# A recurrence kernel's first pass: one unit less between a pair's transposes and its steps, with the prologue's small work moved

## The chip, the cores and the metric

The kernel runs on one core of a Trainium2 chip. The metric is the time of one execution on the device in microseconds (us), the median of repeated runs.

## The reference

The input x is 8 sequences of 1024 tokens with 256 features. Six modulation rows per sequence come from `silu(c) @ wmod` (`sa, ca, ga, sb, cb, gb`). The kernel must compute:

```python
h = layernorm(x) * (1 + ca) + sa
xb = einsum('bsd,ed->sbe', h, B)
# step, over 1024 tokens:
h_t = tanh(h_{t-1} @ A.T + xb_t);  y_t = h_t @ C.T
x = x + ga * layernorm_affine(y + h)
h = layernorm(x) * (1 + cb) + sb
# gated recurrence over 64 groups: f, i = sigmoid(...), g = tanh(...), c = f * c + i * g
x = x + gb * tanh(h @ wo.T + c_final @ uo.T + bo)
```

## The kernel before

Each sequence is cut into 16 chunks of 64 tokens, which gives 128 rows (8 sequences by 16 chunks). One step of the recurrence advances all 128 rows by one token. Tokens go in pairs (`PAIRS` = 32). The first pass handles them in numbered units, and each unit works on several pairs at once, as a pipeline written out by hand in `unit1` of every engine. Engines run their queues in order, and semaphores with counts join them.

For unit number `ref` in the kernel before:

- DVE (VectorE) takes the mean and variance of pair `ref`, and subtracts and scales pair `ref-1` (`hin<-xin,mvA,uvec`, L1071). POOL (GpSimd) works out the reciprocal deviation (L637, L639). ACT (ScalarE) multiplies by it (L808). POOL adds `sa` (L646).
- PE (TensorE) transposes pair `ref-2` into a bank (`psT` or `psC`, L1452), ACT copies pair `ref-3` from its bank, rounded, into `hi` (L784), DVE puts the rest into `lo` (L1083).
- PE multiplies pair `ref-4` by B in twelve matmuls (`times_b`, L1435), in two halves of the accumulators `psWR` or `psOF`. ACT copies the sums to `state` (`xb`, L795).
- PE adds the two steps of pair `ref-R1LAG` (`recur1`, L1400) to the sums, four matmuls a step, and ACT takes the tanh (L763). `R1LAG` is 5, so pair 0 has its first step in unit 5.

A unit on PE is: first step, `times_b`, second step, transposes. Pairs 23 to 31 and the first chunks run in a different order: from unit 28 on (`ahead`), steps are done by `summed` (L1475 on PE, L825 on ACT). ACT then also rounds both steps' results with `high` (`hsh<-hs`, L842), and DVE takes the remainder (`low`, `hsl<-hs,hsh`, L1101). In units 28 and 32 to 35 the eight later weights are transposed as well (`LATE1`, `late`): four transposes on PE (L1361), a copy on ACT (L754), a remainder on DVE (L1029). The second pass follows (`unit2`, `step` at L1489, `project` at L1516), on the same PE queue.

The prologue makes the tables: `ca` and `sa` in two matmuls each (L1335), the weights `B`, `A` and `C` (L1361, L749, `weight_low` at L989), and the other two thirds of the modulation in `batch_rows(1)` and `batch_rows(2)` (L1344, 8 rows by 512 columns, copied by ACT at L811 and L787). SP's queue starts all loads in the order of `FIRST`.

Of the kernel before, what the change touches and what calls it, by code (L numbers as in the profile page):

```python
# [20 lines left out]
def adaln_kernel(nc, x, A, B, C, gamma, beta, wf, uf, bf, wi, ui, bi, wc, uc, bc, wo, uo, bo, in_c, cond, wmod, out):  # L21
# [7 lines left out]
    P = 128  # L29
# [20 lines left out]
    PEELED = 18  # L50
    RAW = 12
    THREE = 8
# [16 lines left out]
    LATE1 = {28: (0,), 32: (1,), 33: (2, 3), 34: (4, 5), 35: (6, 7)}  # L69
# [23 lines left out]
    with ctx:  # L93
# [69 lines left out]
        def htok(p):  # L163

            return hin[:, p % 3 if p < THREE else p % 2, :]

# [27 lines left out]
        def bank(name):  # L194
# [7 lines left out]
        BANK = {"B": psI, "A": psG, "C": psI}  # L202
# [3 lines left out]
        q_table = sem("q_table")  # L206
        q_w = {n: sem("q_w_" + n) for n in EARLY + LATE}
# [37 lines left out]
        a_park = [sem(f"a_park{i}") for i in range(2)]  # L245
        a_park3 = [sem(f"a_park3_{i}") for i in range(3)]
# [77 lines left out]
                    *a_x, *a_xp, a_stats, a_mv, a_ve, a_rstd, a_tmp, a_h, *a_park, *a_park3, a_T, a_hT,  # L324
# [9 lines left out]
        def ranges(cuts, end):  # L334
            return list(zip(cuts, cuts[1:] + [end]))

        RUNS1 = ranges([*range(PEELED), *range(RP1, UNITS1)], UNITS1)

# [114 lines left out]
        def _(sp):  # L453
# [31 lines left out]
            def unit1(v, ref):  # L485
# [4 lines left out]
                if has(ref, 2, PAIRS):  # L490
                    sp.wait_ge(a_h, v.lin(2, -2))
                    p = pair1(v, ref, 2)
                    sp.dma_start(h_park[bass.ds(p * 2, 2), :, :].rearrange("t p d -> p t d"),
                                 two(htok(ref - 2))).then_inc(a_park3[(ref - 2) % 3] if ref - 2 < THREE else a_park[ref % 2], 16)
# [92 lines left out]
            with sp.Fori(0, left) as r:  # L587
# [4 lines left out]
                for i in range(3):  # L592
                    sp.wait_ge(a_park3[i], 16 * len(range(i, THREE, 3)))
                for i in range(2):
                    sp.wait_ge(a_park[i], 16 * ((PAIRS - THREE) // 2))
# [144 lines left out]
        def _(act):  # L740
# [29 lines left out]
            def unit1(v, ref):  # L770
                rec, ahead = has(ref, R1LAG, RP1), ref >= RP1 + R1LAG
                p = ref - RP1 - R1LAG
                if rec:
                    tanhs(v, 0)
                if ref in LATE1:
                    late(LATE1[ref][0])
                if ahead:
                    summed(2 * p)
# [6 lines left out]
                if ref == 4:  # L785
                    act.wait_ge(q_mod, 4)
                    act.activation(mods[:, 2:4, :], psO[0:NB, :].rearrange("b (i d) -> b i d", i=2), ACT.Copy).then_inc(q_col, 1)  # L787
                if has(ref, 4, RP1) or has(ref, 4 + RP1 + AP, PAIRS - RP1 - AP):
                    act.wait_ge(a_B, v.lin(1, -3))
                    if ref - 4 < RP1:  # L790
                        sums = (psWR, psOF)[ref % 2][:, :].rearrange("p (m n) -> p m n", m=H)[:, :, 0:D]
                        xb = row(pair1(v, ref, 4)).rearrange("p (m n) -> p m n", m=H)
                    else:
                        sums, xb = (psW, psO)[ref % 2][:, :], row(pair1(v, ref, 4))
                    act.activation(xb, sums, ACT.Copy).then_inc(a_xb, 1)  # L795
# [13 lines left out]
                if ref == 3:  # L809
                    act.wait_ge(q_mod, 3)  # L810
                    act.activation(mods[:, 0:2, :], psF[0:NB, :].rearrange("b (i d) -> b i d", i=2), ACT.Copy).then_inc(q_col, 1)  # L811
                if ref in (1, 3, 4):
                    weight({1: "B", 3: "A", 4: "C"}[ref])
# [152 lines left out]
        def _(dve):  # L966
            dve.wait_ge(q_ident, 7)
# [3 lines left out]
            def prepare():  # L971
# [60 lines left out]
            def unit1(v, ref):  # L1032
# [19 lines left out]
                if norm:  # L1052
                    dve.wait_ge(a_stats, v.lin(2))
                    if ref >= 2:
                        dve.wait_ge(a_ve, v.lin(1, -1))
                    apart(dve)
                    for tt in range(2):
                        dve.bn_aggr(mv[:, tt, :], st[:, tt, :]).then_inc(a_mv, 1)
                    pair = ref - 1
                    if 3 <= pair < THREE:  # L1060
                        dve.wait_ge(a_T, pair - 2)
                    if pair >= THREE:
                        dve.wait_ge(a_T, v.lin(1, -2))
                    if 3 <= pair < THREE + 2:
                        last = max(p for p in range(min(pair, THREE)) if p % 3 == (pair % 3 if pair < THREE else pair % 2))
                        dve.wait_ge(a_park3[last % 3], 16 * (last // 3 + 1))
                    elif pair >= THREE:
                        dve.wait_ge(a_park[(ref - 1) % 2], v.half(16, 1, -8 * THREE))
# [22 lines left out]
                if ref == 5:  # L1091
                    weight_low(1, "C")
                if ref == 9:
# [234 lines left out]
        def _(pe):  # L1328
            pe.wait_ge(q_ident, 7)
# [9 lines left out]
            def batch_rows(j):  # L1339

                pe.wait_ge(q_wm[f"wm{j}"], 16)
                pe.wait_ge(q_scT, 2)
                for k in range(H):
                    last = pe.matmul((psF, psO)[j - 1][0:NB, :], scT[:, k, :], wm[j][:, k, :], start=(k == 0), stop=(k == H - 1))  # L1344
                last.then_inc(q_mod, 1)

            def batch_columns():

                pe.wait_ge(q_col, 2)
                pe.wait_ge(q_whi, 2)  # L1350
# [14 lines left out]
            def weight(name):  # L1365
                if name == "C":
                    pe.wait_ge(q_whi, 1)
                    pe.wait_ge(q_wlo, 1)
# [13 lines left out]
            def prepare():  # L1382
# [21 lines left out]
            def unit1(v, ref):  # L1404
# [6 lines left out]
                if rec:  # L1411
                    if ref == R1LAG:
                        pe.wait_ge(q_col, 2)
# [4 lines left out]
                def times_b():  # L1418
                    back = 4
                    if not has(ref, back, PAIRS):  # L1420
                        return
                    if ref == back:
                        pe.wait_ge(q_whi, 1)
                        pe.wait_ge(q_wlo, 1)
                    pe.wait_ge(a_hT, v.lin(1, 1 - back))
                    for n in range(3 * H * H):
                        if n == 1:
                            pe.wait_ge(a_hl, v.lin(1, 1 - back))
                        m, k = n // (3 * H), n // 3 % H
                        w, h = ((whi, hmT_hi), (whi, hmT_lo), (wlo, hmT_hi))[n % 3]  # L1430
                        if ref - back < RP1 + AP:
                            ps = sums1(ref - back)[m][:, 0:2 * P]
                        else:
                            ps = (psW, psO)[(ref - back) % 2][:, m * 2 * P:(m + 1) * 2 * P]
                        last = pe.matmul(ps, w["B"][:, k, m * P:(m + 1) * P],  # L1435
                                         h[:, (ref - back) % 2, k * 2 * P:(k + 1) * 2 * P],
# [300 lines left out]
```

## Time and profile before

| what | value |
|---|---|
| median of 3 runs | 567.37 us (567.2 to 567.86) |
| profiled execution, own time | 567.14 us |
| its span in the trace | 565.3 us |
| PE busy | 545.3 us, 96% |
| DVE busy | 382.4 us, 68% |
| ACT busy | 341.2 us, 60% |
| POOL busy | 341.6 us, 60% |

The profiled execution takes 1.84 us more than its span, and the median is 0.23 us above it. "Busy" is the share of the span in which an engine has an instruction in work. A PE that is always busy has no gap between matmuls, and then time can only come from work that is removed or run at a higher clock. PEld is the loading of weights into the array, which runs beside the matmuls. In names, `out<-in` gives the tiles written and read, and L with a number is a line of the kernel.

### The profile page before, as it was taken

The numbers are of one execution on the slowest core, as the hardware profiler recorded it, in microseconds if no ns is written. First come the engines' busy times: TensorE is split into PE (matmuls) and PEld (weight loads), VectorE is DVE, ScalarE is ACT, GpSimd is POOL, SyncE is SP. The second block draws the span as 40 slices with busy tenths as digits, with TensorE's granted clock in tenths as the row PEclk, the third lists the DMA queues.
The fourth block names the chain that finished last, engine by engine and source line by source line (L and its number), as shares of the span: only waits on it lengthen the run. The fifth ranks groups of instructions, "written<-read, shape, count | busy, mean of one in ns | idle before, by whom it ended". The sixth has DMA issues, their size and how long they took to land.

```text
span 565.3 us, 13418 instructions
## 1 busy us (share of the span) xinstructions
PE 545.3 (96%) x4616; PEld 533.8 (94%) x4616; DVE 382.4 (68%) x908; ACT 341.2 (60%) x862; POOL 341.6 (60%) x475
## 2 busy tenths in 40 slices
PE   5999999999989999999999999999999999999992
PEld 2899999999989999999999999999999999999992
DVE  6889888886757655555766666666666677666762
ACT  3777777775456555564665556666655557567550
POOL 4667777660466444354766666677666667677353
PEclk9999999999999999999999999999999999999997
DMA  8566445434243222212233333433333343232334
GB/s 277 157 194 195 150 149 150 134 93 157 89 131 112 67 71 76 70 66 76 66 103 100 106 101 92 123 111 102 95 94 95 94 134 110 76 121 68 86 94 148
DMA packets 58513, 64.09 MB, mean 113 GB/s; under 512 B 5408, under 2 KB 49736, under 8 KB 58448
## 3 DMA queue, kind: packets, MB, share of 16 engines
q1 hardware_dynamic: 58448, 63.26, 36.8%
q8 instruction: 36, 0.59, 0.4%
q14 instruction: 29, 0.24, 0.1%
HBM read 46.44 MB, written 16.81 MB: 112 GB/s over the span
## 4 chain that ended last, share of the span: by engine, by line
PE 86%; POOL 3%; issue 3%; ACT 2%; DVE 2%; DMA 1%; SPq 1%; POOLq 0%; DVEq 0%; ACTq 0%
PE psI L1530 14%; PE psOF L1530 14%; PE psG L1530 13%; PE psWR L1584 7%; PE psWR L1489 7%; PE psWR L1400 4%; PE psWR L1435 4%; PE psOF L1435 4%; PE psOF L1400 3%; PE psOF L1516 3%; PE psC L1516 3%; PE psT L1563 2%; PE psT L1452 1%; PE psC L1452 1%; DMA tA<-rows_d 1%
## 5 line engine op out<-in xcount | busy, mean ns | idle before, releaser
L646 POOL TENSOR_TENSOR hin<-hin,uvec 128x256 f32<-128x256 f32 x64 | 50.7, 813 | 32.5 <-ACT hin L808 32.5
L653 POOL TENSOR_TENSOR hsl<-hs,hsh 128x512 fp32r<-128x512 f32 x24 | 30.9, 1287 | 52.2 <-DVE state L1245 31.6
L881 ACT ACTIVATE psOF<-psOF,biasT 128x256 f32<-128x256 f32 x64 | 25.9, 444 | 56.4 <-PE psOF L1530 56.4
L1229 DVE SCALAR_TENSOR_TENSOR lo<-psT,cb1T,hi 128x256 fp32r<-128x256 f32 x60 | 26.3, 479 | 46.4 <-ACT hi L873 46.4
L1117 DVE TENSOR_TENSOR pre<-psWR,state 128x256 f32<-128x256 f32 x44 | 18.6, 424 | 47.7 <-PE psWR L1489 47.7
L1489 PE MATMUL psWR<-hs,AT 128*128 128x128 f32 x368 | 49.7, 275 | 1.0 <-ACT hs L835 1.0
L660 POOL TENSOR_TENSOR xin<-xin,tA 128x512 f32<-128x512 f32 x32 | 41.5, 1298 | 13.5 <-DMA tA<-rows_d 13.5
L687 POOL TENSOR_TENSOR zn<-zn,tA 128x512 f32<-128x512 f32 x32 | 41.3, 1289 | 12.1 <-ACT zn L846 12.1
L1071 DVE SCALAR_TENSOR_TENSOR hin<-xin,mvA,uvec 128x256 f32<-128x256 f32 x56 | 41.1, 772 | 9.6 <-DMA h_park<-hin 9.2
L846 ACT ACTIVATE zn<-state,nmA,rstdA 128x256 f32<-128x256 f32 x64 | 35.0, 595 | 20.5 <-POOL nmA L677 20.5
L1489 PEld LDWEIGHTS psWR<-hs,AT 128*128 128x128 f32 x368 | 45.3, 191 | 1.4 <-ACT hs L835 1.2
L682 POOL TENSOR_TENSOR wx<-wx,tG 128x512 f32<-128x512 f32 x24 | 36.4, 1518 | 11.0 <-ACT wx L905 10.8
L700 POOL TENSOR_TENSOR wx<-wx,uvec 128x512 f32<-128x512 f32 x24 | 31.0, 1293 | 14.7 <-DVE state L1245 12.6
L846 ACT ACTIVATE xn<-state,nmB,rstdB 128x256 f32<-128x256 f32 x64 | 34.8, 590 | 5.2 <-POOL nmB L709 5.0
L881 ACT ACTIVATE gg<-psG,biasT 128x256 f32<-128x256 f32 x64 | 27.0, 474 | 16.6 <-PE psG L1530 16.6
L835 ACT ACTIVATE hs<-pre 128x256 f32<-128x256 f32 x44 | 18.3, 417 | 29.7 <-DVE pre L1117 29.5
L1530 PE MATMUL psI<-hi,wiT_hi 128*128 128x256 f32 x120 | 35.9, 299 | 0.0
L881 ACT ACTIVATE psI<-psI,biasT 128x256 f32<-128x256 f32 x64 | 26.0, 445 | 14.9 <-PE psI L1530 14.9
L808 ACT ACTIVATE hin<-hin,rstdA 128x256 f32<-128x256 f32 x64 | 28.7, 498 | 9.8 <-POOL rstdA L639 9.8
L1530 PE MATMUL psOF<-hi,wfT_hi 128*128 128x256 f32 x120 | 33.5, 279 | 1.1 <-DVE gf L1165 1.1
L1530 PE MATMUL psI<-lo,wiT_hi 128*128 128x256 f32 x120 | 33.3, 278 | 0.0
L1530 PE MATMUL psOF<-lo,wfT_hi 128*128 128x256 f32 x120 | 33.3, 278 | 0.0
(351 smaller groups left out, 2303.8 us busy)
## 6 DMA issues: line engine op xcount, KB each, us to landing
h_park<-hin SPq DMA_DIRECT2D x32, 256.0 KB, 2.2
hin<-h_park SPq DMA_DIRECT2D x64, 128.0 KB
xin<-in_L_attn_x_dram SPq DMA_DIRECT2D x64, 128.0 KB
tA<-rows_d SPq DMA_DIRECT2D x32, 256.0 KB, 4.5
out_dram<-state SPq DMA_DIRECT2D x64, 128.0 KB
xin<-in_L_attn_x_dram SPq DMA_DIRECT2D x28, 256.0 KB, 2.9
tW<-rows_d SPq DMA_DIRECT2D x32, 128.0 KB, 4.0
tG<-rows_d SPq DMA_DIRECT2D x24, 128.0 KB, 4.0
```

Source lines behind the costliest of these rows:

```text
L646: pool.tensor_tensor(h, h, sa, ALU.add).then_inc(a_h, 1)
L660: pool.tensor_tensor(xg, xg, both(tA[:, m % 2, D:W]), ALU.add).then_inc(s_xg, 1)
L682: pool.tensor_tensor(t, t, both(gb_of(o)), ALU.mult).then_inc(s_ob, 1)
L687: pool.tensor_tensor(two(zn[:, :]), two(zn[:, :]), both(tA[:, m % 2, 0:D]), ALU.mult).then_inc(s_zg, 1)
L846: act.activation(dst[:, j * D:(j + 1) * D], tiles_of(m)[:, j, :], ACT.Identity, bias=nm[:, j:j + 1], scale=rstd[:, j:j + 1]).then_inc(done, 1)
L881: act.activation(dst[:, m * POS:(m + 1) * POS], src[:, m * POS:(m + 1) * POS], fn, bias=biasT[:, i, m, n % NB:n % NB + 1]).then_inc(done, 1)
L1071: dve.scalar_tensor_tensor(halfw(dst, tt), halfw(src, tt), mv[:, tt, 0:1], ca1, ALU.subtract, ALU.mult).then_inc(a_tmp, 1)
L1400: ins = pe.matmul(sums1(v.c - R1LAG)[m][:, tt * P:(tt + 1) * P], AT[:, k, m * P:(m + 1) * P], hs[:, k, :, 1 - tt, :], start=False, stop=(k ...
L1435: last = pe.matmul(ps, w["B"][:, k, m * P:(m + 1) * P], h[:, (ref - back) % 2, k * 2 * P:(k + 1) * 2 * P], start=(n % (3 * H) == 0), stop= ...
L1489: ins = pe.matmul(ps, AT[:, k, m * P:(m + 1) * P], hs[:, k, :, (t - 1) % 4, :], start=(k == 0 and (separate or m == 0)), stop=(k == H - 1 ...
L1530: last = pe.matmul(ps[:, at + m * columns:at + (m + 1) * columns], w[name][:, k, m * P:(m + 1) * P], xx[:, k, :], start=(start and n == 1) ...
L1584: last = pe.matmul(ps[:, j * D:(j + 1) * D], h[:, k, j * P:(j + 1) * P], w["wo"][:, k, :], start=(n < HELD and c == 1 and j == 0), stop=(c ...
```

## The change

`R1LAG` becomes 4: `times_b` and the first step move one unit towards the transposes. Pair `ref-3` is now copied by ACT, completed by DVE and multiplied by PE in the same unit, and the first pass has 35 units in place of 36. `times_b` does the eight matmuls that read `hi` first and the four that read `lo` last. ACT's order in a unit changes. The first pair's means are taken ahead of the wait for `ca`. All pairs use three `hin` buffers, so the loop that covered units 17 to 22 is written out. `batch_rows(1)` moves from unit 2 to 3, `batch_rows(2)` from 3 to 7, the weight C from unit 4 to 6, `batch_columns` from 8 to 9, and the small tables on DVE from units 6 to 15 to units 9 to 18. Seven matmuls without a use (`busy`) are added in the prologue. The weight A is loaded ahead of the two thirds.

```diff
-    R1LAG = 5
-    UNITS1 = PAIRS + 4
+    R1LAG = 4
+    UNITS1 = PAIRS + 3
...
-    FIRST = ["cond", "ca", "x0", "sa", "B", "x1", "x2", "wm1", "A", "x3", "wm2", "x4", "C", "x5"]
+    FIRST = ["cond", "ca", "x0", "sa", "B", "x1", "x2", "A", "wm1", "x3", "x4", "C", "x5", "wm2"]
...
-    LATE1 = {28: (0,), 32: (1,), 33: (2, 3), 34: (4, 5), 35: (6, 7)}
+    LATE1 = {27: (0,), 31: (1,), 32: (2, 3), 33: (4, 5), 34: (6, 7)}
...
-            return hin[:, p % 3 if p < THREE else p % 2, :]
+            return hin[:, p % 3, :]
...
# ACT, unit1
-                if rec:
-                    tanhs(v, 0)
                 if ref in LATE1:
                     late(LATE1[ref][0])
-                if ahead:
-                    summed(2 * p)
                 if has(ref, 3, PAIRS):
...
                     act.activation(hmT_hi[:, b, :], (psT, psC)[b][:, :], ACT.Copy).then_inc(a_hT, 1)
...
+                if ref == 3:
+                    weight("A")
+                if rec:
+                    tanhs(v, 0)
                 if ahead:
-                    summed(2 * p + 1)
-                    high(p)
-                if rec:
-                    tanhs(v, 1)
-                if ref == RP1 + R1LAG - 1:
-                    starts()
+                    summed(2 * p)
                 if has(ref, 1, PAIRS):
...
+                if has(ref, 3, RP1) or has(ref, 3 + RP1 + AP, PAIRS - RP1 - AP):
...
+                    act.activation(xb, sums, ACT.Copy).then_inc(a_xb, 1)
+                if rec:
+                    tanhs(v, 1)
+                if ahead:
+                    summed(2 * p + 1)
+                    high(p)
+                if ref == RP1 + R1LAG - 1:
+                    starts()
...
+                if ref in (4, 8):
+                    i = (4, 8).index(ref)
+                    act.wait_ge(q_mod, 3 + i)
+                    act.activation(mods[:, 2 * i:2 * i + 2, :], psI[0:NB, :].rearrange("b (i d) -> b i d", i=2), ACT.Copy).then_inc(q_col, 1)
...
# DVE
+            dve.memset(pre[:, :], 1.0).then_inc(q_pre, 1)
...
+                dve.wait_ge(a_stats, 2)
+                apart(dve)
+                for tt in range(2):
+                    dve.bn_aggr(mv[:, tt, :], st[:, tt, :]).then_inc(a_mv, 1)
...
-                if 6 <= ref < 16:
-                    tables(ref - 6)
+                if 9 <= ref < 19:
+                    tables(ref - 9)
...
# PE
+            def busy(n):
+
+                for _ in range(n):
+                    pe.matmul(psT[:, 0:P], pre[:, 0:P], pre[:, 0:P], start=True, stop=True)
+
+            pe.wait_ge(q_pre, 1)
+            busy(4)
...
+                busy(1)
                 pe.wait_ge(q_scT, 1)
                 table("ca", psC[:, D:W], D)
+                busy(2)
                 table("sa", psO[:, 0:D], 0)
...
+                    pe.wait_ge(a_hT, v.lin(1, -2))
+                    for n, (m, w, h, k) in enumerate([(m, w, hmT_hi, k) for m in range(H) for w in (whi, wlo) for k in range(H)] +
+                                                     [(m, whi, hmT_lo, k) for m in range(H) for k in range(H)]):
+                        if n == 2 * H * H:
+                            pe.wait_ge(a_hl, v.lin(1, -2))
...
                 times_b()
+                if ref == 3:
+                    batch_rows(1)
...
                 if ref == 2:
-                    batch_rows(1)
                     weight("A")
-                if ref == 3:
+                if ref == 6:
+                    weight("C")
+                if ref == 7:
                     batch_rows(2)
-                if ref == 4:
-                    weight("C")
-                if ref == 8:
+                if ref == 9:
                     batch_columns()
```

PE's queue in the prologue, from the first pair's transposes to the first step (`psG<-ident,state` is the weight A, `psI<-ident,state` the weight C, `psOF<-state` and `psI<-state` the two thirds, `psWR<-hs,AT` the first step). Before:

```order
L1452 MATMUL psT<-ident,hin 128x128 [waits a_h]
L1452 MATMUL psT<-ident,hin 128x128
L1344 MATMUL psOF<-state 8x512 [waits q_scT,q_wm_wm1]
L1361 MATMUL psG<-ident,state 128x128 [waits q_w_A]
L1452 MATMUL psC<-ident,hin 128x128 [waits a_h]
L1344 MATMUL psOF<-state 8x512 [waits q_scT,q_wm_wm2]
L1435 MATMUL psWR<-hi,chi 128x256 [waits a_hT,q_wlo,q_whi]
L1435 MATMUL psWR<-lo,chi 128x256 [waits a_hl]
L1452 MATMUL psT<-ident,hin 128x128 [waits a_h,a_hl,a_hT]
L1361 MATMUL psI<-ident,state 128x128 [waits q_w_C,q_wlo,q_whi]
L1400 MATMUL psWR<-hs,AT 128x128 [waits q_whi,a_xb,a_end,q_col]
```

These are the rows at which a wait stands or a new group starts. After:

```order
L1453 MATMUL psT<-ident,hin 128x128 [waits a_h]
L1453 MATMUL psT<-ident,hin 128x128
L1366 MATMUL psG<-ident,state 128x128 [waits q_w_A]
L1435 MATMUL psWR<-hi,chi 128x256 [waits a_hT,q_wlo]
L1435 MATMUL psWR<-lo,chi 128x256 [waits a_hl]
L1349 MATMUL psI<-state 8x512 [waits q_scT,q_wlo,q_wm_wm1]
L1453 MATMUL psC<-ident,hin 128x128 [waits a_h]
L1406 MATMUL psWR<-hs,AT 128x128 [waits a_xb,q_whi,a_end]
```

The third pair's transposes, the weight C and the second third have left the stretch ahead of the first step, and `times_b` of the first pair now stands ahead of the first third.

ACT's queue where one unit of the `ahead` part meets the next, at the second later weight (`wiT_hi`). `hsh<-hs` is `high`, `hs<-psWR` and `hs<-psOF` are tanhs, `hi<-psT` and `hi<-psC` the copy for `times_b`. Before:

```order
L825 ACTIVATE hs<-psWR 128x8x16 [waits s_r,s_hsl]
L825 ACTIVATE hs<-psWR 128x8x16 [waits s_r]
L842 ACTIVATE hsh<-hs 128x16x32 [waits s_tanh]
L808 ACTIVATE hin<-hin,rstdA 128x256 [waits a_tmp,a_rstd]
L808 ACTIVATE hin<-hin,rstdA 128x256 [waits a_tmp]
L754 ACTIVATE wiT_hi<-psI 128x512 [waits q_lT]
L825 ACTIVATE hs<-psOF 128x8x16 [waits s_r,s_hsl]
L825 ACTIVATE hs<-psOF 128x8x16 [waits s_r]
L784 ACTIVATE hi<-psC 128x512 [waits a_B,a_T]
```

After:

```order
L820 ACTIVATE hs<-psWR 128x8x16 [waits s_r,s_hsl]
L820 ACTIVATE hs<-psWR 128x8x16 [waits s_r]
L837 ACTIVATE hsh<-hs 128x16x32 [waits s_tanh]
L750 ACTIVATE wiT_hi<-psI 128x512 [waits q_lT]
L776 ACTIVATE hi<-psT 128x512 [waits a_B,a_T]
L820 ACTIVATE hs<-psOF 128x8x16 [waits s_r,s_hsl]
L820 ACTIVATE hs<-psOF 128x8x16 [waits s_r]
L788 ACTIVATE hin<-hin,rstdA 128x256 [waits a_tmp,a_rstd]
L788 ACTIVATE hin<-hin,rstdA 128x256 [waits a_tmp]
```

The copy now stands right behind `high` and the weight's copy, ahead of the next tanh and of the scaling. It serves the `times_b` of its own unit, where it served the next unit's before.

## Rows read from the trace of the kernel before

**Rows 1.** Busy time of each engine in three stretches, PE's granted clock.
```profile
10.00:20.00 10.00, 9.53 (x40) 4.23 (x40) 9.49 (x24) 5.08 (x12) 7.27 (x12) 0.83 0.79 249
60.00:70.00 10.00, 10.00 (x90) 10.00 (x89) 8.26 (x22) 7.97 (x24) 7.06 (x11) 1.00 0.50 160
110.00:120.00 10.00, 10.00 (x90) 10.00 (x89) 8.90 (x20) 7.44 (x23) 7.59 (x12) 1.00 0.52 149
```
**Rows 2.** Chain that ended last, prologue, in order of time: start, us, what.
```profile
4.34 2.06 PE psC L1335 x4
...
7.93 0.84 POOL rstdA L639
...
10.91 0.44 PE psT L1452 x2
11.35 3.46 PE psOF L1344 x4
...
15.83 1.81 PE psOF L1344 x4
17.65 1.62 PE psWR L1435 x12
19.27 0.44 PE psT L1452 x4
19.71 0.44 PE psI L1361 x4
```
**Rows 3.** PE in short stretches of the prologue: busy, granted clock.
```profile
5.00:5.70 0.70, 0.70 (x3) 1.00 0.93 262
11.40:12.00 0.60, 0.60 (x1) 0.50 1.07 416
14.50:15.00 0.50, 0.50 (x3) 0.72 0.68 242
```
**Rows 4.** Timeline of the prologue: start, us, engine, instruction, idle before and releaser.
```profile
3.30 0.47 SPq L472 DMA_DIRECT2D xin<-in_L_attn_x_dram  x1
4.88 0.75 DVE L981 BATCH_NORM_STATS2 stA<-xin 128x6 f32<-128x256 f32 x2 [0.61 <-DMA xin<-in_L_attn_x_dram]
9.05 0.75 DVE L1046 BATCH_NORM_STATS2 stA<-xin 128x6 f32<-128x256 f32 x2
12.12 0.67 DVE L989 TENSOR_TENSOR clo<-psI,chi 128x512 fp32r<-128x512 f32 x1
14.51 0.68 DVE L1083 TENSOR_TENSOR lo<-psT,hi 128x512 fp32r<-128x512 f32 x1
```
**Rows 5.** Loads of the first 18 us: count, size, median us to landing.
```profile
xin<-in_L_attn_x_dram SPq DMA_DIRECT2D x2, 256.0 KB, 4.3
```
**Rows 6.** Timeline of a unit that starts at 64.43.
```profile
63.99 0.60 PE L1452 MATMUL psT<-ident,hin 128*128 128x128 f32 x4
64.43 1.06 PE L1400 MATMUL psWR<-hs,AT 128*128 128x128 f32 x8
65.22 0.19 PEld L1435 LDWEIGHTS psOF<-hi,chi 128*128 128x128 f32 x1
```
**Rows 7.** Timeline of an `ahead` unit that starts at 112.27.
```profile
111.83 0.60 PE L1452 MATMUL psC<-ident,hin 128*128 128x128 f32 x4
112.03 0.28 ACT L825 ACTIVATE hs<-psWR 128x128 f32<-128x128 f32 x1 [0.17 <-PE psWR L1475]
112.34 0.63 ACT L842 ACTIVATE hsh<-hs 128x512 fp32r<-128x512 f32 x1
112.88 0.89 ACT L808 ACTIVATE hin<-hin,rstdA 128x256 f32<-128x256 f32 x2
113.99 0.59 ACT L784 ACTIVATE hi<-psC 128x512 fp32r<-128x512 f32 x1
114.59 1.05 PE L1475 MATMUL psOF<-hs,AT 128*128 128x128 f32 x8
```
**Rows 8.** Timeline at two `late` weights.
```profile
122.78 0.68 DVE L1029 TENSOR_TENSOR wiT_lo<-psI,wiT_hi 128x512 fp32r<-128x512 f32 x1
123.38 0.68 DVE L1101 TENSOR_TENSOR hsl<-hs,hsh 128x512 fp32r<-128x512 f32 x1
128.38 0.60 ACT L754 ACTIVATE ufT_hi<-psI 128x512 fp32r<-128x512 f32 x1
128.87 0.59 ACT L754 ACTIVATE uiT_hi<-psG 128x512 fp32r<-128x512 f32 x1
```

More of the change, by code:

```diff
@@ L244, in adaln_kernel @@
         a_h = sem("a_h")
-        a_park = [sem(f"a_park{i}") for i in range(2)]
-        a_park3 = [sem(f"a_park3_{i}") for i in range(3)]
+        a_park = [sem(f"a_park{i}") for i in range(3)]
         a_T = sem("a_T")
@@ L334, in ranges @@
         def ranges(cuts, end):
-            return list(zip(cuts, cuts[1:] + [end]))
-        RUNS1 = ranges([*range(PEELED), *range(RP1, UNITS1)], UNITS1)
+            return list(zip(cuts, [*cuts[1:], end]))
+        RUNS1 = ranges(range(UNITS1), UNITS1)
         def walk(eng, runs, unit):
@@ L493, in unit1 @@
                     sp.dma_start(h_park[bass.ds(p * 2, 2), :, :].rearrange("t p d -> p t d"),
[L494 removed]
+                                 two(htok(ref - 2))).then_inc(a_park[(ref - 2) % 3], 16)
                 for what in LOADS.get(ref, []):
@@ L592, in _ @@
                 for i in range(3):
-                    sp.wait_ge(a_park3[i], 16 * len(range(i, THREE, 3)))
-                for i in range(2):
-                    sp.wait_ge(a_park[i], 16 * ((PAIRS - THREE) // 2))
+                    sp.wait_ge(a_park[i], 16 * len(range(i, PAIRS, 3)))
                 sp.wait_ge(a_T, PAIRS)
@@ L1051, in unit1 @@
                     late(i)
-                if norm:
+                if norm and ref >= 2:
                     dve.wait_ge(a_stats, v.lin(2))
-                    if ref >= 2:
-                        dve.wait_ge(a_ve, v.lin(1, -1))
+                    dve.wait_ge(a_ve, v.lin(1, -1))
                     apart(dve)
@@ L1058, in unit1 @@
                         dve.bn_aggr(mv[:, tt, :], st[:, tt, :]).then_inc(a_mv, 1)
+                if norm:
                     pair = ref - 1
-                    if 3 <= pair < THREE:
+                    if pair >= 3:
                         dve.wait_ge(a_T, pair - 2)
[L1062 to L1068, printed above, removed]
+                        dve.wait_ge(a_park[pair % 3], 16 * (pair // 3))
                     for tt in range(2):
@@ L1341, in batch_rows @@
                 pe.wait_ge(q_wm[f"wm{j}"], 16)
-                pe.wait_ge(q_scT, 2)
+                if j == 1:
+                    pe.wait_ge(q_wlo, 1)
+                    pe.wait_ge(q_scT, 2)
+                else:
+                    pe.wait_ge(q_col, 1)
                 for k in range(H):
-                    last = pe.matmul((psF, psO)[j - 1][0:NB, :], scT[:, k, :], wm[j][:, k, :], start=(k == 0), stop=(k == H - 1))
+                    last = pe.matmul(psI[0:NB, :], scT[:, k, :], wm[j][:, k, :], start=(k == 0), stop=(k == H - 1))
                 last.then_inc(q_mod, 1)
@@ L1418, in times_b @@
                 def times_b():
-                    back = 4
-                    if not has(ref, back, PAIRS):
+                    q = ref - 3
+                    if not has(ref, 3, PAIRS):
                         return
-                    if ref == back:
-                        pe.wait_ge(q_whi, 1)
+                    if q == 0:
                         pe.wait_ge(q_wlo, 1)
[L1425 to L1436, printed above, removed]
-                                         start=(n % (3 * H) == 0), stop=(n % (3 * H) == 3 * H - 1))
+                    pe.wait_ge(a_hT, v.lin(1, -2))
[3 more added lines that the diff above has]
+                            pe.wait_ge(a_hl, v.lin(1, -2))
+                        last = pe.matmul(sums1(q)[m][:, 0:2 * P], w["B"][:, k, m * P:(m + 1) * P], h[:, q % 2, k * 2 * P:(k + 1) * 2 * P],
+                                         start=(n % (2 * H) == 0 and n < 2 * H * H), stop=(n >= 2 * H * H and k == H - 1), skip_group_check=True)
                     last.then_inc(a_B, 1)
                 times_b()
+                if ref == 3:
+                    batch_rows(1)
                 if rec:
```

40 lines of the change are left out of this document (14 added, 26 removed).

## The prediction

> **What bounds the kernel now.** I read the busy time by stretch first. From 60 to 70 and from 110 to 120 us PE is busy for 10.00 of 10 us, with 90 matmul records each time, at the full granted clock (1.00, the 2.4 GHz level) [rows 1]. DVE has 8.3 to 8.9 of 10, ACT 7.4 to 8.0, POOL 7.1 to 7.6. So in the whole first pass PE never waits: its own work is the bound, and a unit lasts what its matmuls last. The reader is to take from this that a pipeline with less lag cannot make a unit shorter. It can only change how long PE sits idle ahead of the first full unit, and it can bring in waits that were not there.
>
> Then I read the chain in the prologue. PE is on it without a break from 10.91 [rows 2]: transposes of the first pair, the first third 3.46, the weight A, the second pair, the second third 1.81, `times_b` 1.62, the third pair 0.44, the weight C 0.44. The first step starts at 19.71 + 0.44 = 20.15. The first third costs 3.46 and the second 1.81 for the same four records, since the granted clock is 0.50 from 11.4 (the 1.2 GHz level), is on its way back at 14.5 to 15.0 with 0.72, and PE had gaps before it fell [rows 3]. So the stretch from 10.91 to 20.15 holds 3.46 - 1.81 = 1.65 us of avoidable time and no idle at all.
>
> **The change, part by part: the start.** What is moved behind the first step is not removed: the second third (1.81), the third pair's transposes (0.44) and the weight C (0.44) [rows 2]. PE owes these 2.69 us later, in units that are full. The first step must therefore start before 20.15 - 2.69 = 17.46 for the start to gain anything.
>
> When can it start? The means ahead of `ca` take the reciprocal deviation off the chain (it ended at 7.93 + 0.84 = 8.77 [rows 2]), and the first pair is transposed some 1.2 us earlier. But `times_b` of the first pair needs `lo`, which DVE makes at 14.51, behind the second and third pair's means and scaling in its own queue. That queue starts with the second pair's means at 9.05 [rows 4]. They read the load x1, issued at 3.30. The median time to landing of the first two x loads is 4.3 [rows 5], and the first took 4.88 - 1.82 = 3.06 (issue to the end of DVE's wait), so x1 took about 5.5 and landed near 8.85. DVE can gain 0.2 us at most there, and I take `lo` from 14.4 to 15.1. `times_b` can run its eight `hi` matmuls from 12.12 + 0.67 = 12.79 on, when the remainder of B is there [rows 4]; it then waits for `lo`.
>
> PE now idles from about 10.5 to 12.8 and again ahead of 15.1, because the work that filled this stretch has moved away. At the 1.2 GHz level the four `lo` matmuls take 4 x 0.24 = 0.95 (twice 1.43/12 each), and the first third starts at 16.05. I let the clock come back near 16.3, behind steady work as it did before. Then the third ends at 18.0, the second pair's transposes at 18.5, and with the hand-off the first step starts at 18.6. The start costs 2.69 - (20.15 - 18.6) = **1.15 us**. Bounds: if the clock never falls, `lo` at 15.1, four matmuls 0.48, the third 1.73, transposes 0.44 give 17.75 and a cost of 0.3. If it stays low through the third, 16.05 + 3.46 + 0.5 gives 20.0 and 2.55. I take the middle, nearer to the row of 11.4, where it fell after smaller gaps.
>
> The Trainium skill (TensorE: Matmul & The Clock Gate, section What's actually happening) says that the default state is throttled and that activity releases the throttle. By that rule the seven `busy` matmuls would bring `ca` and `sa` to full speed and, with the clock kept up, the start's cost would be the 0.3 above. The trace agrees that it falls after gaps, but its clock column shows 1.00 at 5.0 to 5.7 [rows 3], where four records of `ca` need 2.06 us, so at the very start it does not tell the level.
>
> **The steady units.** In units 4 to 26 the copy of pair `ref-3` (0.59 [rows 7]) must lie between the transposes at the end of one unit and `times_b` in the next. Transposes end at 63.99 + 0.60 = 64.59, the copy could run from 64.63 to 65.22 and PE sees it near 65.27 (0.05 for a hand-off). PE loads the first weights of `times_b` at 65.22 [rows 6]. So the copy is late by about 0.05, in 22 units: **1.1 us**. Bounds: 0, since the difference is smaller than a hand-off is known, and 0.15 a unit, if the weight load (0.19) is no longer hidden: 3.3 us. In units 4 and 8 ACT copies a third at the unit's end, one slot of 0.49 [rows 8], ahead of the next copy: about 0.3 each, **0.6 us**. `lo` is read eight matmuls later (8 x 0.12 = 0.95), which covers DVE's 0.68. DVE's other work (tables, the C remainder) stays within its free time. The third buffer only removes DVE's waits, and PE does not wait for DVE. `busy` lies in idle time.
>
> **The ahead units.** Here the copy meets `high`. Let S be PE's start of a unit, 112.27. ACT's tanh of the last step runs to 112.31, `high` starts at 112.34 and the next slot opens at 112.88 [rows 7]. Before, that slot went to the scaling and the copy ran at 113.99 for the next unit. Now the copy takes the slot: 112.88 + 0.59 + 0.05 = 113.52. PE wants to begin `times_b` at 114.59 - 1.43 = 113.16. It waits 0.36. This is a chain by order: tanh, `high`, copy after the last step of a unit, against transposes and one step on PE. The three units without a late weight (28 to 30): 3 x 0.36 = 1.08.
>
> With one late weight in front (units 27, 31, 32), ACT's copy of it takes another slot, 128.87 - 128.38 = 0.49 [rows 8]: the pair's copy is ready at 114.01. PE has 0.44 more work ahead, so wants it at 113.60: 0.41. Then DVE: its remainder of the late weight starts at 112.88 + 0.60 + 0.04 = 113.52, `low` follows 0.60 later (123.38 - 122.78 [rows 8]), `lo` at 114.72, done and seen at 115.45. PE wants it 0.95 into `times_b`, at 114.96: another 0.49. Together 0.90, three times: 2.70. Units 33 and 34 have the second late weight of the unit before as well, so ACT's two copies end later (S + 1.79 against 1.33: 0.46) and DVE has one more remainder (S + 3.33 against 2.74: 0.59): 2 x 1.05 = 2.10. Sum **5.9 us**. In unit 27 there is no `high` ahead but the boundary copy on DVE, which I count the same. Bounds: 3.2 if DVE is never late (3 x 0.36 + 3 x 0.41 + 2 x 0.46), 7 if the waits add to each other.
>
> PE is the bound before and behind these places, so each wait is lost. Loads of the second pass are freed about 2 us later relative to its start, and I see no PE wait that they end; I count nothing. If that cover is gone they cost up to that 2 us.
>
> **Sum.** 567.14 + 1.15 + 1.1 + 0.6 + 5.9 = 575.9 us. The profiled execution is 0.23 under the median of the runs, which I leave within the error.
>
> **The rivals.** (a) Faster: the earlier first pair carries through. If DVE's queue is not held by x1 but moves with the first pair, `lo` comes 1.25 earlier, at 13.85, and with the clock up the first step starts at 13.85 + 0.48 + 1.73 + 0.44 = 16.5. That gains 3.65 - 2.69 = 0.96 and gives 566.2, if no wait comes in later. It decides only while all later waits stay below 1 us. For it speaks that the steady margin is within 0.05, against it the ahead chain, 0.3 too long even without a late weight. (b) The lag does not matter: waits and the start's gain cancel, or ACT's slots fall so that the copy is in time, 567.1. Against it again the order on ACT. (c) Only the copy is late, DVE is not, and the start costs nothing: 567.14 + 3.2 = 570.3. For it speaks that DVE's slots are worked out from a unit in which nothing waited for it. (d) Worse: clock and DVE both at their bad ends, 567.14 + 2.55 + 3.3 + 0.6 + 7 = 580.6.
>
> **How the numbers follow.** The forecast (571 to 580, slower) has 0.60, (a) 0.17, (b) 0.08, (c) 0.12, (d) 0.03. The likeliest alone runs from 567.14 + 0.3 + 0.6 + 3.2 = 571.2 to 580. For 8 in 10 the range leaves out (a) and (d): 566.5 to 580. Within 0.2% (1.1 us) is what a measurement of this kernel cannot tell from no change; faster has 0.17, same 0.08, slower 0.75.
>
> **What would show it.** In the profile after: waits of PE for `hi` (ACT, L776) and for `lo` (DVE, L1077), which before had none, each some 0.4 us in the seven or eight `ahead` units; PE busy under 10.00 in 10 us windows between 100 and 140; the first step near 18.6 with PE idle between 10 and 15; the stretch of granted clock 0.50 in the prologue at another place. The prediction is wrong if the first step starts before 17.4, or if PE stays at 10.00 through the `ahead` units.

## The result, and the profile after

The changed kernel takes 577.19 us (median of 5 runs, 576.29 to 578.27), against 567.37 us before (565.73 to 567.86 over 5 runs). The ratio is 1.0183, 95% interval 1.0168 to 1.0199. The profiled execution took 576.29 us with a span of 574.4, 9.1 more than the span of 565.3 before.

Busy time in stretches of 10 us, the changed kernel (columns as in [rows 1]; the last stretch has no row there):

```profile
10.00:20.00 10.00, 7.91 (x39) 5.03 (x40) 7.30 (x18) 4.50 (x11) 6.38 (x11) 0.83 0.80 260
60.00:70.00 10.00, 10.00 (x89) 10.00 (x88) 8.82 (x24) 7.79 (x22) 7.28 (x11) 1.00 0.47 138
110.00:120.00 10.00, 9.63 (x83) 9.25 (x82) 7.49 (x22) 6.14 (x18) 6.83 (x12) 1.00 0.41 129
130.00:140.00 10.00, 8.85 (x71) 8.06 (x70) 4.38 (x7) 5.55 (x16) 1.43 (x2) 1.00 0.08 27
```

In the steady units PE is as full as before. In the `ahead` units it has 83 matmul records where it had 90 [rows 1], and 71 where two late weights lie in one unit. What it waited for between 100 and 145 us (us in total, times, the longest one) says on whom:

```profile
PE psWR L1435 <- ACT hi L776: 1.1, 4, 0.3
PE psOF L1435 <- ACT hi L776: 1.0, 4, 0.3
PE psOF L1435 <- DVE lo L1077: 0.5, 2, 0.3
PE psWR L1435 <- DVE lo L1077: 0.5, 2, 0.3
```

Eight waits for `hi`, one a unit, and four for `lo`. From 20 to 100 us the list is empty.

The chain that ended last, in the prologue (answers to [rows 2]):

```profile
13.76 0.61 DVE lo L1077
14.37 0.04 issue
14.41 1.22 PE psWR L1435 x4
15.64 2.49 PE psI L1349 x4
18.13 0.59 PE psC L1453 x4
18.72 0.89 PE psWR L1406 x8
```

Before, this chain stood on PE alone from 10.91 on. Now DVE is on it up to 14.37, and PE's first step comes at 18.72 where it came at 20.15 (19.71 + 0.44).

**Where the 9.1 us are.** I take four marks on PE: the first step, the start of the first `ahead` unit (that of its late transposes), the first `project` and the first step of the second pass. These are starts in the timeline, where the first step stands 0.1 to 0.2 ahead of its place in the chain. The first two were at 20.05 and 104.55, and are now at 18.55 and 107.12. The first step of the second pass went from 142.58 to 151.97, 9.39 later. From `project` to there both kernels take the same (6.32 and 6.31).

- Start: the first step is 1.50 earlier, 2.69 of work is owed, so it costs 1.19.
- Steady units: 88.57 in place of 84.50, less the 2.25 of moved work that now lies there (C 0.44, second third 1.81): 1.82.
- `ahead` units: 38.54 up to `project` (145.66) in place of 31.71 (136.26), less the 0.44 of transposes: 6.39.

These add up to 9.40. The second pass gives 0.3 back in this pair of executions.

Inside the `ahead` stretch the timeline shows the mechanism. First a unit without a late weight, its first step starting at S = 115.86:

```profile
115.43 0.60 PE L1453 MATMUL psT<-ident,hin 128*128 128x128 f32 x4
115.86 1.06 PE L1475 MATMUL psOF<-hs,AT 128*128 128x128 f32 x8
115.94 0.63 ACT L837 ACTIVATE hsh<-hs 128x512 fp32r<-128x512 f32 x1
116.47 0.58 ACT L776 ACTIVATE hi<-psT 128x512 fp32r<-128x512 f32 x1
117.10 0.51 PE L1435 MATMUL psWR<-hi,chi 128*128 128x256 f32 x2 [0.18 <-ACT hi L776]
117.21 0.68 DVE L1077 TENSOR_TENSOR lo<-psT,hi 128x512 fp32r<-128x512 f32 x1
118.16 0.64 PE L1435 MATMUL psWR<-lo,chi 128*128 128x256 f32 x4
```

The transposes were done at 116.03. The copy waits for `hsh`, ends at 117.05, and PE starts 0.05 later, at S + 1.24 (worked out before: 1.25). A full step takes 0.89, so `times_b` is 0.35 late. Its eight `hi` matmuls then take 1.06 and not the 0.95 that four pairs of 0.24 make, so the unit lasts 4.10, where its work is 3.65. The extra 0.10 lies in the first two, which take 0.34. In the kernel before the first matmul of `times_b` is long too (0.20 against 0.12), but it starts at S + 0.81 (113.08), 0.08 before the step is through, and so costs nothing. PE's wait is written as 0.18 in the row above, and the unit loses 0.45: the waits listed for PE add up to 3.1 us, and the loss below is twice that. The loss is to be read from the length of the unit.

Then a unit in which the copies and remainders of two late weights lie ahead of the pair's own:

```profile
134.94 0.60 ACT L750 ACTIVATE ufT_hi<-psI 128x512 fp32r<-128x512 f32 x1
135.44 0.59 ACT L750 ACTIVATE uiT_hi<-psG 128x512 fp32r<-128x512 f32 x1
135.91 0.60 ACT L776 ACTIVATE hi<-psT 128x512 fp32r<-128x512 f32 x1
136.18 0.68 DVE L1029 TENSOR_TENSOR uiT_lo<-psG,uiT_hi 128x512 fp32r<-128x512 f32 x1
136.57 0.51 PE L1435 MATMUL psWR<-hi,chi 128*128 128x256 f32 x2 [0.34 <-ACT hi L776]
136.78 0.68 DVE L1095 TENSOR_TENSOR hsl<-hs,hsh 128x512 fp32r<-128x512 f32 x1
137.38 0.68 DVE L1077 TENSOR_TENSOR lo<-psT,hi 128x512 fp32r<-128x512 f32 x1
138.11 0.75 PE L1435 MATMUL psWR<-lo,chi 128*128 128x256 f32 x4 [0.32 <-DVE lo L1077]
```

PE waits twice: 0.34 for the copy, third in ACT's row, and 0.32 for `lo`, third behind two remainders on DVE. The eight units last 4.64, 4.10, 4.10, 4.11, 5.11, 5.56, 5.72 and 5.20. Their work is 4.09, three times 3.65, 4.09, 4.53, 4.53 and 4.09. The waits and the longer first matmuls behind them are 0.55, 0.45 (three times), 1.02, 1.03, 1.19 and 1.11, 6.25 of the 6.39. The rest is that the units of the kernel before took 0.13 less than the same sum of work.

The steady stretch, in the chain of the changed kernel:

```profile
23.32 1.68 PE psWR L1435 x12
...
27.22 1.49 PE psOF L1435 x12
...
30.04 0.44 PE psG L1366 x4
30.48 0.89 PE psOF L1406 x8
31.37 1.43 PE psWR L1435 x12
```

`times_b` takes 1.49, where it took 1.43. But behind the four transposes of the weight C, which give ACT 0.44 more, it takes 1.43 again, and 1.42 behind the second third. Where ACT has copied a third just before, it takes 1.68. The unit with the second third lasts 5.66, 0.20 more than 3.65 + 1.81.

### The profile page after: what moved, and what is told of

The parts are those of the page before. It is cut to its first block, busy times and chain, and to the rows that moved or that the text cites. A ratio compares the mean times of both kernels' runs of the same rounds, so it can differ in the third digit from the quotient of the medians.

```text
span 574.4 us, 13239 instructions
## 1 busy us (share of the span) xinstructions
PE 553.0 (96%) x4630; PEld 539.6 (94%) x4630; DVE 376.4 (66%) x909; ACT 343.8 (60%) x862; POOL 340.5 (59%) x475
## 4 chain that ended last, share of the span: by engine, by line
PE 84%; DVE 3%; ACT 3%; issue 3%; POOL 2%; DMA 1%; SPq 1%; POOLq 0%; DVEq 0%; ACTq 0%
PE psI L1530 14%; PE psOF L1530 13%; PE psG L1530 13%; PE psWR L1584 7%; PE psWR L1489 7%; PE psWR L1435 4%; PE psOF L1435 4%; PE psWR L1406 4%; PE psOF L1406 3%; PE psOF L1516 3%; PE psC L1516 3%; PE psT L1563 2%; DMA tA<-rows_d 1%; PE psC L1453 1%; PE psT L1453 1%
## 5 line engine op out<-in xcount | busy, mean ns | idle before, releaser
L642 POOL TENSOR_TENSOR hin<-hin,uvec 128x256 f32<-128x256 f32 x64 | 47.3, 760 | 37.8 <-ACT hin L788 37.8
L696 POOL TENSOR_TENSOR wx<-wx,uvec 128x512 f32<-128x512 f32 x24 | 31.0, 1293 | 14.5 <-DVE state L1239 12.4
L1530 PE MATMUL psI<-hi,wiT_lo 128*128 128x256 f32 x120 | 33.3, 277 | 0.0
```

Source lines behind the costliest of these rows:

```text
L642: pool.tensor_tensor(h, h, sa, ALU.add).then_inc(a_h, 1)
L1530: last = pe.matmul(ps[:, at + m * columns:at + (m + 1) * columns], w[name][:, k, m * P:(m + 1) * P], xx[:, k, :], start=(start and n == 1) ...
```

## The experiments

Each ratio is to the kernel before, measured on the same chip. On the first chip that took 566.17 us, on the second 566.50, on the third 566.07. The changed kernel itself, on the second chip (e0_changed_again):

> The changed kernel once more, as the reference for the others on one chip: 1.018 times the kernel before. The prologue differs between executions: where the clock is low through the whole first third, the first step starts at 19.5 to 20.5 us in place of 18.6 and the time is 1 to 2 us longer.

577.48 us, ratio 1.0189 (1.0166 to 1.0212). Its first step came at 18.90 in the timeline.

### Who is late in the `ahead` units

**The pair's copy and remainder first** (e1_copy_first). On ACT and DVE:

```diff
+                if has(ref, 3, PAIRS):
+                    act.wait_ge(a_T, v.lin(1, -2))
+                    if ref >= 5:
+                        act.wait_ge(a_B, v.lin(1, -4))
+                    b = (ref - 3) % 2
+                    act.activation(hmT_hi[:, b, :], (psT, psC)[b][:, :], ACT.Copy).then_inc(a_hT, 1)
+                if ahead and p > 0:
+                    high(p - 1)
+                for i in LATE1.get(ref - 1, ())[1:]:
+                    late(i)
                 if ref in LATE1:
                     late(LATE1[ref][0])
-                if has(ref, 3, PAIRS):
...
-                    act.activation(hmT_hi[:, b, :], (psT, psC)[b][:, :], ACT.Copy).then_inc(a_hT, 1)
...
```

On DVE `hmT_lo` is moved ahead of `late` and `low` in the same way.

> The changed kernel with the pair's copy first in ACT's unit (then the rounding of the unit before, then the late weights' copies) and the pair's remainder first on DVE. If the ahead units lose their time to the order on ACT and DVE, PE's eight ahead units fall from 6.3 us over their work to 0.5 (0.06 each, the hand-off), and the time is about 577.2 - 5.8 = 571.4. If something else holds these units (the loads of the second pass, the clock, contention), it stays at 575 or more.

Measured: 571.62 us, ratio 1.0080 (1.0056 to 1.0103). Its 110 to 120 and 130 to 140 us:

```profile
110.00:120.00 10.00, 10.00 (x88) 10.00 (x88) 8.44 (x22) 7.29 (x22) 6.69 (x11) 1.00 0.46 135
130.00:140.00 10.00, 10.00 (x90) 10.00 (x89) 5.96 (x10) 7.01 (x20) 1.79 (x2) 1.00 0.15 49
```

and one unit, with S = 112.90:

```profile
113.10 0.60 ACT L774 ACTIVATE hi<-psC 128x512 fp32r<-128x512 f32 x1 [0.16 <-PE psC L1457]
113.60 0.62 ACT L838 ACTIVATE hsh<-hs 128x512 fp32r<-128x512 f32 x1
113.73 0.69 DVE L1075 TENSOR_TENSOR lo<-psC,hi 128x512 fp32r<-128x512 f32 x1 [0.19 <-ACT hi L774]
113.76 0.50 PE L1439 MATMUL psOF<-hi,chi 128*128 128x256 f32 x2
```

The same instructions in another order: ACT now waits for the transposes, and PE starts at S + 0.86. The list of PE's waits is empty from 100 to 150, and the excess of the eight units is 0.2 where it was 6.4 (32.34 from the first `ahead` unit to `project`). The ratio fell by 0.0103 to 0.0109, 5.8 to 6.2 us, where the intervals allow some 1.6 us either way. So the order on ACT and DVE is the `ahead` term, all of it. The two spans differ by only 3.4, since this execution has its first step 1.8 later and its second pass 1.1 longer.

**Only the remainder first** (e2_lo_first: the DVE half of that edit).

> The changed kernel with the pair's remainder ahead of the late weight's remainder and of the steps' remainder on DVE alone; ACT is as in the changed kernel. Order theory: the waits of PE for the remainder in units 31 to 34 go (0.48, 0.48, 0.59, 0.59 = 2.1 us by the trace), the waits for the copy stay, the time is about 575.1. Rival: DVE's work only moves and the steps' remainder is late instead: 577.2, or more.

Measured: 576.26 us, ratio 1.0164 (1.0141 to 1.0187). What PE waited for from 100 to 150 us:

```profile
PE psWR L1435 <- ACT hi L776: 1.1, 4, 0.3
PE psOF L1435 <- ACT hi L776: 1.0, 4, 0.3
```

The waits for `lo` are gone, those for `hi` are as they were. The last four units became 0.47, 0.48, 0.61 and 0.60 shorter, 2.16 in sum. The time fell by 0.0019 to 0.0025 of it, 1.1 to 1.4 us, half of what was expected, though the intervals don't exclude 2.1. In its profiled execution the first step was 1.2 us later and the second pass 1.2 longer than in that of the changed kernel, which hides the 2.16 there. DVE's share of the term is thus 2.2, and ACT's, by subtraction, about 4.2. No run has ACT's half of the edit alone.

### The steady units

**Only the order of `times_b`'s matmuls, in the kernel before** (e8_matmul_order). The start and stop flags follow the order. In this kernel the two halves of the last pair lie in one bank, and in this order they are open together. Its results are changed, which I put down to that pair (no run shows it). Every instruction is there.

```diff
-                    for n in range(3 * H * H):
-                        if n == 1:
+                    for n, (m, w, h, k) in enumerate([(m, w, hmT_hi, k) for m in range(H) for w in (whi, wlo) for k in range(H)] +
+                                                     [(m, whi, hmT_lo, k) for m in range(H) for k in range(H)]):
+                        if n == 2 * H * H:
                             pe.wait_ge(a_hl, v.lin(1, 1 - back))
...
```

> The kernel before with only the order of the twelve matmuls changed (eight that read hi, then four that read lo). The steady units of the changed kernel take 3.71 us against 3.65. If that is the hand-off from the copy, this order costs nothing here, where the copy is a unit ahead: 0.999 to 1.001. If the order itself costs 0.06 a unit, 31 units cost 1.9 us: 1.003.

Measured: 566.24 us, ratio 0.9998 (0.9986 to 1.0011). Its `times_b` in the chain:

```profile
57.08 1.43 PE psOF L1434 x12
```

The order of the matmuls costs nothing; the 1.9 us that it would cost at 0.06 a unit lie outside the interval. What remains of 1.49 against 1.43 is then the hand-off from ACT's copy, as the units with 0.44 more work ahead of it suggest. No run removed it alone.

### The start

**The first pair's means ahead of `ca`, in the kernel before** (e3_means_first), **and that with the seven `busy` matmuls** (e4_means_busy).

```diff
                 for tt in range(2):
                     dve.bn_stats(st[:, tt, :], halfw(xin[:, 0, :], tt)).then_inc(a_stats, 1)
+                dve.wait_ge(a_stats, 2)
+                apart(dve)
+                for tt in range(2):
+                    dve.bn_aggr(mv[:, tt, :], st[:, tt, :]).then_inc(a_mv, 1)
...
```

> The kernel before with the first pair's means ahead of the wait for the table, nothing else. If PE's saturated queue starts earlier it gains what the first pair gains, up to 1.1 us (566.3). If the first third's load (landing near 11.3) or DVE's queue holds it, nothing: 567.2. I expect 0.3 us gained.

> The run before with the seven matmuls without a use added. If they keep the clock at its upper level until the first third, it takes 1.8 us in place of 3.5 and the time is 1.6 us lower than without them (about 565.5). If the clock falls in the gaps after them anyway, they change nothing (within 0.3 us).

Measured: 0.9991 (0.9978 to 1.0004) and 0.9994 (0.9983 to 1.0005). In the profiled execution of e3_means_first the first third took 3.51 and the first step stood at 20.63 in the chain. In that of e4_means_busy it stood at 19.32. The medians, 565.88 and 566.23 us, don't follow: with `busy` in, the time is no lower. The 1.6 us of a first third at full clock did not come; a gain under 1 us is not excluded, nor is the 0.3 us that I expected of the means resolved.

**The changed kernel without `busy`** (e7_no_busy: the three calls and the wait for `pre` taken out).

> The changed kernel without its seven matmuls without a use. Theory 1 (they do not release the clock in a way that the time shows, as the kernel before with them in gave no difference): the time stays at that of the changed kernel, ratio 1.017 to 1.019 to the kernel before. Theory 2 (they keep the clock up, as the page on TensorE's clock would have it): without them ca and sa and what follows run at half rate longer and the time is 0.5 to 2 us higher, ratio 1.020 to 1.022.

Measured: 577.17 us, ratio 1.0202 (1.0186 to 1.0219). That is 0.0013 to 0.0019 above the changed kernel's, with intervals that overlap. By its number it lies in the range of the second theory, that `busy` keeps the clock up. Its third took 2.90 (2.49 there, 1.90 in e0_changed_again). So an effect of about 1 us stays open here; in the kernel before none was seen. The traces add one thing. In the nine executions with `busy` the first clock record of 1.00 begins between 6.7 and 10.2 us. In the five without it begins at 7.7, 7.95, 10.2, 14.5 and 15.15, and the two late ones (e10_before_x_first and e3_means_first) have a first third of 3.2 and 3.5 us. Two of five against none of nine is too few to call it shown.

**The first third back ahead of the first step** (e5_third_early): loaded ahead of A, done in unit 2 in a bank of its own (`psF`). ACT copies it a unit earlier, and the second pair's `times_b` waits for that copy, as it uses the same bank.

```diff
-    FIRST = ["cond", "ca", "x0", "sa", "B", "x1", "x2", "A", "wm1", "x3", "x4", "C", "x5", "wm2"]
+    FIRST = ["cond", "ca", "x0", "sa", "B", "x1", "x2", "wm1", "A", "x3", "x4", "C", "x5", "wm2"]
...
-                if ref == 3:
-                    batch_rows(1)
...
                 if ref == 2:
+                    batch_rows(1)
                     weight("A")
...
```

> The changed kernel with the first third back in unit 2, in a bank of its own, ahead of the weight A, and its load ahead of A's. If the start loses because PE idles from 10.5 to 12.8 and up to 14.4 us while the third waits behind, the third now lies in that gap even at the low clock, the first step starts near 17.3, 1.3 to 3 us earlier than in the changed kernel, and the time falls by about 2 us. If the first step is held by DVE's queue or by the clock alone, it stays.

Measured: 575.06 us, ratio 1.0142 (1.0121 to 1.0164), 2.4 us under the changed kernel on that chip. The two kernels in the middle of the prologue, first the changed one:

```profile
14.00:15.00 1.00, 0.86 (x4) 0.59 (x3) 1.00 (x3) 0.38 (x1) 0.59 (x1) 0.50 1.04 366
15.00:16.00 1.00, 1.00 (x4) 0.45 (x4) 0.39 (x4) 0.85 (x3) 0.79 (x2) 0.50 0.61 138
```

then e5_third_early:

```profile
14.00:15.00 1.00, 0.95 (x8) 0.74 (x7) 1.00 (x2) 0.48 (x1) 0.92 (x3) 1.00 0.73 261
15.00:16.00 1.00, 0.64 (x5) 0.64 (x6) 0.96 (x3) 0.43 (x2) 0.53 (x1) 1.00 0.72 239
```

With the third in the hole where PE waited 1.9 us for `hi`, the granted clock stays at 1.00 (2.4 GHz) where it was 0.50 (1.2 GHz). The first step comes at 17.10. All other traces agree: the five executions of this lag with the third behind have a stretch of 0.50 that begins between 12.8 and 15.4 us, and the four with the third early (this one, and three below) have none in the prologue. The gain is of both, the filled gap and the clock; no run separates them. The profiled execution is the longest of this kernel's four (576.58), and there a stretch of 0.50 came in the second pass instead, from 170.5 us.

### Both together, and the loads of the second pass

**e1 and e5 in one kernel** (e6_both, and once more as e6_both_again):

> Both repairs, the pair's copy and remainder first (e1) and the third early (e5). If the two losses are independent: the changed kernel less 6 less 2 us, 1.004 times the kernel before or 568.5. If the second pass's loads, freed late in this version, bind instead, about 1 us more.

> e6_both once more beside e9_both_x_first: ratio 1.0034 within 0.0008. It fixes the difference of the two to some 0.3 us on one chip.

Measured: 568.59 us, ratio 1.0034 (1.0023 to 1.0045), and 568.34 us, 1.0033 (1.0020 to 1.0046). By the marks, its first step at 17.08, first `ahead` unit at 105.54, `project` at 137.89: start -0.28, steady units 1.71, `ahead` 0.20, 1.63 in sum. The steady units are nearly all that is left.

But POOL started on the second pass's first x only 1.6 us behind that pass's first step, where before it was 2.85 ahead. So I also let SP issue these loads ahead of its waits for the parked h (e9_both_x_first on e6_both, e10_before_x_first on the kernel before):

```diff
+                sp.wait_ge(a_tmp, 2 * PAIRS)
+                sp.wait_ge(q_rows, 16)
+                load_x(0)
+                load_x(1)
                 for i in range(3):
                     sp.wait_ge(a_park[i], 16 * len(range(i, PAIRS, 3)))
...
```

> e6_both, with the second pass's first loads of x and tA issued by SP as soon as pair 31 is scaled, ahead of its waits for the parked h. In e6_both POOL started on xin (L656) 1.6 us behind the second pass's first step (in the kernel before 2.85 ahead of it), and PE waited 1.4 us for xn in two places against 0.7 in one. Theory 1 (the lost cover of these loads costs something): POOL starts on xin at least 2 us ahead of the first step, the waits for xn fall from 1.4 to 0.7 or less, and the time falls by 0.7 to 1.1 us, to a ratio of about 1.002 to the kernel before. Theory 2 (the loads' cover costs nothing, e6_both's 0.34% is spread over the first pass): POOL's start moves but the ratio stays at 1.0034 within 0.0005.

> The kernel before with the same earlier loads of x and tA. Here POOL started on xin 2.85 us ahead of the second pass's first step, and PE waited 0.7 us once for xn. Theory 1 (the cover matters only where it is missing): no change, ratio 1.000 within 0.001. Theory 2 (the loads hold up the second pass's start in every kernel, the 0.7 is theirs): 0.7 us less, ratio 0.9988, and then e9_both_x_first's gain says nothing about the lag.

Measured: 568.65 us, 1.0043 (1.0030 to 1.0056), and 566.92 us, 1.0008 (0.9997 to 1.0019). POOL's row for that x, in e6_both_again and then in e9_both_x_first:

```profile
145.34 1.29 POOL L656 TENSOR_TENSOR xin<-xin,tA 128x512 f32<-128x512 f32 x1 [15.44 <-DMA tA<-rows_d]
```

```profile
135.59 1.27 POOL L656 TENSOR_TENSOR xin<-xin,tA 128x512 f32<-128x512 f32 x1 [7.12 <-DMA tA<-rows_d]
```

The load moved from 0.5 behind the second pass's first step (144.86) to 7.8 ahead of it (143.43), and the median did not fall. My theory that the lost cover costs 0.7 to 1.1 us of it fell.

The profiles don't say that the cover is free, though. PE's wait for `xn`, in e6_both and in e6_both_again:

```profile
PE psT L1567 <- ACT xn L842: 1.4, 2, 0.8
PE psT L1567 <- ACT xn L842: 0.8, 1, 0.8
```

POOL began on that x 1.6 us behind the first step in the first, and 0.5 behind in the second. It was 1.2 behind in e1_copy_first and e2_lo_first, and these have the second wait too (1.2, 2 times). In the ten other executions it was ahead, and none has it. So the second wait goes with the place of that load: by these rows there is slack up to somewhere between 0.5 and 1.2 us, and past it PE waits 0.5 to 0.7 more, 11 us into the second pass. That e9_both_x_first gained nothing fits, as its neighbour e6_both_again was within the slack. How often an execution passes it, and so what it costs the median, stays open. No kernel of the shorter lag beats the kernel before; the best of them stands at 1.0033.

## Why the prediction was right, step by step

**What bounds the kernel.** Right. Behind the prologue PE has no free time in the first pass, so every wait that the shorter lag brought in is in the total. No wait was there to be removed.

**The `ahead` units, 5.9.** Right in mechanism, place and nearly in size: 6.4. The plain unit was put at 0.36 and took 0.45. `times_b` is 0.35 late, and 0.10 more is lost in its first matmul, which now starts behind a wait, a term that I did not have. Unit 27 was put at 0.90 and took 0.55, since DVE's remainder was in time there: my "which I count the same" was wrong. The units with late weights were put at 0.90 and 1.05 and took 1.02 to 1.19. DVE is late only in four units, where I had five. Its part of 2.2 was shown apart (e2_lo_first), and ACT's 4.2 is the rest.

**The steady units, 1.1 + 0.6.** Measured 1.8: 0.06 in most units, 0.25 and 0.22 behind ACT's copies of a third, and 0.20 in the unit that got the second third, which I had not counted. The 1.1 rested on a difference of 0.05 between two rows of the trace, and that held.

**The start, 1.15.** The profiled execution says 1.19, but by errors that cancel, so the agreement is luck. I had `lo` begin at 14.4 and end at 15.1, since x1 would land near 8.85. DVE ran the second pair's means already at 8.46 and `lo` at 13.68:

```profile
8.46 0.75 DVE L1046 BATCH_NORM_STATS2 stA<-xin 128x6 f32<-128x256 f32 x2
...
13.68 0.68 DVE L1077 TENSOR_TENSOR lo<-psT,hi 128x512 fp32r<-128x512 f32 x1
```

So `lo` was there at 14.36, 0.7 earlier than I had it, though not at the 13.85 that rival (a) needed. What it gained was lost to the clock, which fell behind the gap: the four `lo` matmuls took 1.22 where I had 0.95, and the third 2.49 where I had 1.95 and (a) 1.73. For (a) `ahead` was too long anyway. One execution is also a thin base for this term. Of the five executions of this lag with the third behind, the chain has the first step at 18.72, 19.06, 19.26, 19.91 and 20.53, mean 19.50. In the five with the old lag it stands at 19.02, 19.32, 20.14, 20.30 and 20.63, mean 19.88. By these means the start costs 2.69 - 0.38 = 2.3. I take that as an estimate, since the kernels differ in other ways. With it the terms sum to 10.5, and the medians stand 9.8 and 11.0 us above the kernel before (577.19 and 577.48).

**The loads of the second pass, counted at nothing.** POOL's first x went from 2.85 ahead of the first step (139.73) to 0.23 ahead (151.74), so they are 2.6 later relative to it where I had said 2. For this kernel counting them at nothing was right: its two profiled executions, and that without `busy`, have POOL 0.1 to 0.4 ahead, and none has the second wait for `xn`. It was close. With the `ahead` units repaired the same load falls 0.5 to 1.6 behind, and part of the price that I had named as an upper bound appears.

**The Trainium skill's rule on the clock.** I had taken the `busy` matmuls to bring the start's cost down to 0.3, if the clock stays up. It did not: in each of the five executions with the third behind it fell, in the gap of 1.9 us or within 2 us after it. Their gain was not seen in the kernel before (0.9994 against 0.9991), and about 1 us of it stays open in the changed one (1.0202 without). What kept the clock up was real work in the gap (e5_third_early). The Trainium skill ("TensorE: Matmul & The Clock Gate", section "What's actually happening") says that activity releases the throttle. These traces agree so far as e5_third_early goes: with matmuls in the gap the granted clock stayed at 1.00.

## What to carry to other kernels

A shorter lag moves work nearer to its consumer, and pays only where the bounding engine waits. With that engine full, ask of each step which row of the helper's queue now lies between producer and consumer, and sum those rows: here one copy placed behind a rounding and up to two weights' copies, and its remainder behind theirs, cost 6 us of the 9, and putting both first gave them back. A margin of a twentieth of a microsecond in a loop is worth reading, as it comes back once a unit. And a hole made in a prologue can cost twice, by its length and by the clock. A view that lists waits tells where they are; what they cost is the length of the unit against its work.

## What the runs showed of the hardware

- The prologue differs from one execution to another. In two executions of the changed kernel the first third (four matmuls of 8 rows by 512 columns) took 2.49 and 1.90; in kernels of the old lag it took 3.46, 3.51, 3.21 (e10_before_x_first) and 1.88 (e8_matmul_order). The first step moves with it, by up to 1.8 us among executions of one lag (18.72 to 20.53 with the third behind).
- The clock column does not always tell. In e3_means_first it shows 1.00 while two matmuls fill the whole microsecond, part of the third that took 3.51:

```profile
12.00:13.00 1.00, 1.00 (x2) 0.14 (x1) 1.00 (x5) 0.69 (x2) 0.38 (x2) 1.00 1.06 396
13.00:14.00 1.00, 1.00 (x2) 0.14 (x1) 1.00 (x4) 0.69 (x2) 1.00 (x2) 1.00 1.09 378
```

  The trace's clock records begin only at 15.15 us there, and the column shows 1.00 where it has none. In the kernel before they begin at 7.95, so the 1.00 at 5.0 to 5.7 [rows 3] is no measurement either.

- The first two matmuls behind a wait take 0.34 us where two take 0.24 (1.06 for eight, where eight take 0.95). Without a wait the first one is nearly as long, but starts 0.08 before the group ahead of it is through.
- The clock can fall without a change in the kernel. In the second pass every execution has a gap of 0.9 to 1.0 us and one of 0.75 on PE, 2 us apart. In one of fourteen (e5_third_early) a stretch of 0.50 followed, and its second pass took 424.3 us, where those without the second wait for `xn` have 422.2 to 423.0.
